# Row maxima and shift of the first causal group inside the project stage, x loaded further ahead, and the local attention's window loop written out

## The chip, the cores and the metric

The kernel runs on one core of one Trainium2 chip. The metric is the device time of one execution in microseconds (us); of several executions the median counts.

## The reference, cut to what matters

The input x has shape (4, 1024, 256). It is normalised, and the normalised rows xn go two ways: through a causal attention of 16 heads of 16 columns, and through two layers of a local attention (window 128, look-back of one window, 8 heads of 64) with a gated feed-forward. The result is x plus the product of the first with silu of the second.

```python
xn = layernorm(x)
s = causal_attention(xn, W_q, W_k, W_v, W_o)
h = xn
for l in range(2):
    h = h + local_attention(shift(h) @ wqkv[l]) @ wo[l]
    a, g = split(norm(shift(h)) @ w1[l] + b1[l])
    h = h + (a * gelu(g)) @ w2[l] + b2[l]
out = x + s * silu(h)
```

Both attentions need, for each row of scores, its maximum before the exponential. What stands below turns on those of the causal attention.

## The kernel before

The program runs stage after stage: `phase_project`, `phase_causal`, then `phase_window` and `phase_feed` for each of two layers. In each stage every engine has its own list of instructions, written out by hand, which it works through strictly in order; semaphores join the lists. A stage is a block: no engine enters the next one before all have left it.

**Project (lines 81 to 360).** The 4096 tokens are cut into 8 supers of 512. For super s, VectorE (DVE) takes moments of the rows of super s + 2 (`moments`, L275, L279) and normalises those of super s + 1 (`normalise`, L285); TensorE (PE) turns the rows (`transposes`, L331), ScalarE (ACT) copies them (L250), and DVE takes the rounding remainder (`lo_of`, L291). Then for each of four groups g of heads PE makes queries and keys with six matmuls into its own bank of `pQ` (L345). These are split into three bf16 parts in a chain: ACT copies the first part (L258), DVE subtracts it (L308, `p_rest`), ACT copies the second (L260), GpSimd (POOL) subtracts the third (L206). After the four groups PE makes the values with 24 matmuls (L356) into `pV`, two banks, which DVE copies out (L317, two copies). The queue of SyncE (SP) stores the parts to `QKP` (L152), the normalised rows to `X` (L146) and the values to `VA` (L157), and loads the rows of super s + 2 (L172). It also fills the operands of the first causal group, `ca_qs`, `ca_ks` and `ca_vin`: 13 transfers (`stack_transfers`), of which four go out after each of supers 2, 3 and 4, and one after super 5 (`first_group`, L167).

**Causal (from line 363).** There are 16 groups, each one batch and four heads. A group needs its 48 row maxima first: a bf16 matmul of up to 512 columns into one of three banks `ca_pR` (`maxima`, L549), then one DVE instruction that keeps the maximum (`take_max`, L691 for a chunk without a mask, L687 with one). `MAXJOBS` lists them: eight query tiles from the last to the first, four heads, one or two chunks of keys. DVE then splits the maxima into two bf16 parts (`split`, L697 to L701), PE turns them (`turn_shift`, L561), DVE copies them out (L706), and two small transfers place them as two extra rows of `ca_qs` (`place_shift`, L508). Only then can PE make scores that already hold the shift (`scores`, L573), of which ACT takes the exponential (L659). For groups 1 to 15 the maxima are spread through the steps of the group before. Those of group 0 stand alone at the head of the stage, in `first`, with the first nine of group 1 (`NEARLY`) behind them. POOL sets `ca_ks`'s two rows of ones and the pad of `ca_va` at the head of the stage (L463 to L467).

**Window (from line 804).** 32 windows per layer. Every engine but DVE runs 24 of them in a loop of three passes over eight windows, and the last eight written out:

```python
    def steps(e, step):
        with e.Fori(0, NW // TPB - 1) as it:
            for j in range(TPB):
                step(it * TPB + j, j, it)
        for j in range(TPB):
            step(NW - TPB + j, j, NW // TPB - 1)
```

DVE has all 32 written out. A pass ends in a branch backwards, so each layer has two. In the windows with j = 0, the first of a batch, the look-back block is left out. PE turns the rows of a later window once in each (`turn_h`, L1230), and opens a window with 18 matmuls (`project`, L1252).

## Time and profile before

| what | us |
|---|---|
| median of 3 executions (1977.71 to 1978.39) | 1978.15 |
| the profiled execution's own time | 1978.07 |
| its span in the trace | 1976.2 |
| project stage and the change of stage, to the first causal matmul | 112.36 |
| from there to the first causal scores | 35.16 |
| causal stage after that, to the first window matmul | 483.6 |
| PE busy | 1839.4 |
| DVE busy | 1502.2 |
| ACT busy | 1208.0 |
| POOL busy | 988.4 |

The own time is what the clock outside measured for the profiled execution; the span reaches from the first to the last instruction in the trace. Busy shares are sums over the whole run. In rows of the trace "L308" is a line of the code, the name left of "<-" is written and those right of it are read, "xN" merges N equal instructions, and what stands in square brackets at the end is the time that the engine sat idle just before and what released it.

### The profile page before, as it was taken

Reading aid. Unit: us, or ns where it says so; the run is one execution under the profiler, and the core shown is the slowest. Engines: PE = TensorE matmul, PEld = TensorE weight load, DVE = VectorE, ACT = ScalarE, POOL = GpSimd, SP = SyncE. Lnnn points to the kernel's source line nnn. Section 1 sums busy time; section 2 is a strip of 40 time slices with the busy share of each in tenths; the row PEclk is TensorE's granted clock in tenths of the full one; section 3 lists DMA queues with packets and bytes.
Section 4 is the critical chain, followed back from the end, with each engine's and each line's share of the span. In section 5 each row is a group of like instructions: output and inputs, shape, how many; then the busy total and the mean of one; then the engine's idle time right before and its main releaser. Section 6 shows DMA issues by size and latency. Waiting matters only on the chain. (4 is left out here: it accounts for less than half of the span.)

```text
span 1976.2 us, 38537 instructions
## 1 busy us (share of the span) xinstructions
PE 1839.4 (93%) x12768; PEld 1314.2 (66%) x12768; DVE 1502.2 (76%) x4131; ACT 1208.0 (61%) x2523; POOL 988.4 (50%) x801
## 2 busy tenths in 40 slices
PE   6879999999998899999997899979999999789999
PEld 5723333333333687878886788868888888668888
DVE  5778888888881998989996555369999999855654
ACT  3516666666666677777775433447777777644553
POOL 3532223222222777767773433357777777443433
PEclk9969999999998899999998999989999999989999
DMA  6993456456430000000022112110000001232222
GB/s 208 308 194 44 66 68 84 60 74 78 59 44 23 14 28 24 25 28 28 28 74 69 61 57 65 44 35 24 26 27 27 27 27 28 63 117 85 71 69 86
DMA packets 142299, 126.87 MB, mean 64 GB/s; under 512 B 31091, under 2 KB 124719, under 8 KB 141999
## 3 DMA queue, kind: packets, MB, share of 16 engines
q1 hardware_dynamic: 140782, 123.36, 27.2%
q8 instruction: 96, 1.57, 0.3%
q10 hardware_dynamic: 1344, 1.31, 0.2%
q14 instruction: 77, 0.62, 0.1%
HBM read 82.41 MB, written 41.96 MB: 63 GB/s over the span
## 5 line engine op out<-in xcount | busy, mean ns | idle before, releaser
L659 ACT ACTIVATE ca_pr<-ca_pS 128x1024 f32<-128x1024 f32 (+3 forms) x384 | 296.6, 811 | 207.2 <-PE ca_pS L573 166.6
L488 POOL TENSOR_SCALAR_AFFINE_SELECT ca_pr<-ca_pr 128x256 f32<-128x256 f32 x256 | 103.7, 409 | 372.9 <-ACT ca_pr L659 368.8
L687 DVE CUSTOM_DVE_ANT_0 ca_masked<-ca_pR,ca_later 128x256 f32<-128x256 f32 (+3 forms) x512 | 235.9, 485 | 43.2 <-PE ca_pR L549 39.4
L549 PE MATMUL ca_pR<-ca_ks,ca_qs 96*128 96x512 bf16 (+3 forms) x768 | 220.6, 345 | 9.1 <-DVEq L743 5.7
L573 PE MATMUL ca_pS<-ca_qs,ca_ks 98*128 98x512 bf16 (+3 forms) x768 | 184.8, 332 | 10.5 <-issue 5.3
L691 DVE TENSOR_REDUCE ca_mx<-ca_pR 128x1 f32<-128x512 f32 x256 | 175.7, 686 | 24.8 <-PE ca_pR L549 23.0
L549 PEld LDWEIGHTS ca_pR<-ca_ks,ca_qs 96*128 96x128 bf16 x768 | 70.7, 98 | 165.0 <-DVE ca_mx L687 90.6
L909 POOL TENSOR_TENSOR wb_tsn<-wb_qk,wb_tab 128x512 f32<-128x512 f32 x62 | 133.4, 2173 | 71.1 <-DVE wb_pn L1127 71.1
L594 PE MATMUL ca_pO<-ca_pr,ca_va 128*32 128x512 f32 (+3 forms) x1536 | 166.0, 504 | 1.2 <-POOL ca_pr L488 0.8
L909 POOL TENSOR_TENSOR w_tsn<-w_qk,w_tab 128x512 f32<-128x512 f32 x62 | 129.0, 2101 | 76.0 <-DVE w_pn L1127 67.3
L985 ACT ACTIVATE w_pe<-w_sm,w_nmax 128x256 f32<-128x256 f32 (+1 forms) x256 | 123.2, 483 | 66.7 <-DVE w_nmax L1117 66.4
L985 ACT ACTIVATE wb_pe<-wb_sm,wb_nmax 128x256 f32<-128x256 f32 (+1 forms) x256 | 123.2, 483 | 63.8 <-DVE wb_nmax L1117 63.8
L573 PEld LDWEIGHTS ca_pS<-ca_qs,ca_ks 98*128 98x128 bf16 x768 | 62.5, 98 | 114.1 <-ACT ca_pr L659 68.2
L1127 DVE TENSOR_SCALAR w_pn<-w_pe,w_rsum 128x256 f32<-128x256 f32 (+1 forms) x256 | 97.2, 442 | 2.3
L1127 DVE TENSOR_SCALAR wb_pn<-wb_pe,wb_rsum 128x256 f32<-128x256 f32 (+1 forms) x256 | 95.9, 437 | 2.3
L917 POOL TENSOR_TENSOR wb_rs<-wb_ssc,mhalf 128x16 f32<-128x16 f32 x32 | 94.0, 2939 | 2.7
L917 POOL TENSOR_TENSOR w_rs<-w_ssc,mhalf 128x16 f32<-128x16 f32 x32 | 93.9, 2936 | 2.7
L1117 DVE CUSTOM_DVE_ANT_0 wb_sm<-wb_pS,masks 128x256 f32<-128x256 f32 (+1 forms) x256 | 88.6, 403 | 8.7 <-PE wb_pS L1348 8.7
L1117 DVE CUSTOM_DVE_ANT_0 w_sm<-w_pS,masks 128x256 f32<-128x256 f32 (+1 forms) x256 | 88.6, 403 | 8.4 <-PE w_pS L1348 8.3
L1252 PE MATMUL w_pX<-big_hi,w_thi 128*128 128x512 f32 x192 | 79.3, 413 | 4.3 <-issue 4.3
L1527 POOL TENSOR_TENSOR f_alo<-f_af,f_ahi 128x512 fp32r<-128x512 f32 x40 | 52.6, 1320 | 61.3 <-ACT f_ahi L1584 61.3
L1527 POOL TENSOR_TENSOR fb_alo<-fb_af,fb_ahi 128x512 fp32r<-128x512 f32 x40 | 52.7, 1323 | 58.1 <-ACT fb_ahi L1584 58.1
(293 smaller groups left out, 5417.7 us busy)
## 6 DMA issues: line engine op xcount, KB each, us to landing
QKP<-p_parts SPq DMA_DIRECT2D x32, 384.0 KB, 5.2
ca_qs<-QKP SPq DMA_DIRECT2D x96, 128.0 KB, 6.5
ca_ks<-QKP SPq DMA_DIRECT2D x96, 128.0 KB, 7.0
w_xt<-X SPq DMA_DIRECT2D x64, 128.0 KB, 2.1
X<-w_x SPq DMA_DIRECT2D x64, 128.0 KB, 1.7
f_hh<-X SPq DMA_DIRECT2D x32, 256.0 KB, 6.2
p_xin<-x SPq DMA_DIRECT2D x8, 512.0 KB, 5.7
X<-p_xn SPq DMA_DIRECT2D x8, 512.0 KB, 4.9
```

The costliest lines, as they stand in the source:

```text
L549: pe.matmul(bank[:, 0:w], qs[0:SHIFT_ROW, u, h, i * P:(i + 1) * P], ks[0:SHIFT_ROW, u, h, k0:k0 + w], start=True, stop=True).then_inc(ring ...
L573: ins = pe.matmul(pS[:, pair, hh, 0:w], ks[:, u, h, j * P:(j + 1) * P], qs[:, u, h, q0:q0 + w], start=True, stop=True)
L594: ins = pe.matmul(pO[h * VW:(h + 1) * VW, o:o + w], va[:, u, j, h * VW:(h + 1) * VW], pr[:, k % 2, h // 2, h % 2, 0:w], start=j == 0, stop ...
L659: act.activation(pr[:, k % 2, pair, :, 0:w], pS[:, pair, :, 0:w], ACT.Exp, scale=CS).then_inc(p_ready, 1)
L687: dve.tensor_tensor_reduce(masked[:, jb % RING, 0:w], pR[jb % RING][:, 0:w], later[:, 512 - w:512], -1.0, BIG, ALU.add, ALU.min, mx[:, i, ...
L691: dve.tensor_reduce(mx[:, i, h, ch:ch + 1], pR[jb % RING][:, 0:w], AX.X, ALU.max, negate=True).then_inc(ring_free, 1)
L909: pool.tensor_tensor(*sines(w, j, z), ALU.mult).then_inc(S["ts_ready"], 1)
L917: pool.tensor_tensor(rs[:, j % 2], ssc[:, :], K.mhalf[:, :], ALU.pow).then_inc(S["rs_ready"], 1)
L985: ins = act.activation(pe_[:, h, 0:keys], sm[:, n, 0:keys], ACT.Exp, bias=nmax[:, n:n + 1], scale=-1.0, accum_out=sums[:, h:h + 1])
L1117: ins = dve.tensor_tensor_reduce(sm[:, n, 0:keys], pS[:, n // 2, n % 2, 0:keys], masks[:, j % 2, 0:keys], -1.0, BIG, ALU.add, ALU.min, nma ...
L1127: ins = dve.tensor_scalar(pn[:, h, 0:keys], pe_[:, h, 0:keys], rsum[:, h:h + 1], None, ALU.mult)
L1527: pool.tensor_tensor(alo[:, j, ch], af[:, ch % 2], ahi[:, j, ch].bitcast(F32), ALU.subtract)\
```

## The change

- In the project stage the 48 maxima of group 0 are made during supers 3 to 7, 10 in each and 8 in the last. They are dealt over the four groups g of a super as 3, 2, 3, 2 (2 each in the last), each lot behind the queries and keys of its g on PE, and behind `p_rest` of its g on DVE. They use the two banks of `pV`. PE waits before the first for all 13 transfers of group 0, before each maximum for the bank to be read by the maximum two before it, and before the value matmuls of a super for all its maxima to be read.
- The two copies of the values out of `pV` move from DVE to ACT, behind the last of the four groups.
- After the last super DVE splits the maxima, PE turns them, DVE copies them, and SP places the two rows.
- SP issues seven of the 13 transfers of group 0 inside super 2 and six behind it, and the same for group 1 at super 4. The causal stage's head then loads group 2 alone.
- x has six blocks for its rows (two of its own, four borrowed from buffers of later stages), and five more supers are loaded at the start.
- POOL sets one slot of the rows of ones after each of supers 0, 1 and 2, and the pad of `ca_va` after super 3.
- `steps` of the window stage has no loop: all 32 windows are written out for every engine, in both layers.

The diff, cut to its core:

```diff
@@ -39,6 +39,8 @@
...
+NJ = len(MAXJOBS)
 LOADS = 2 * len(PAIRS) + 1
 
 LAYERS = 2
@@ -78,9 +80,11 @@
...
-def phase_project(nc, K, W, x, X, QKP, VA, wqk, wv):
-
-    FIRST_AT, FIRST_TURNS = 2, 4
+def phase_project(nc, K, W, F, x, X, QKP, VA, wqk, wv):
+
+    LOAD_AT = {2: 0, 4: 1}
+    MAX_AT = 3
+    PER = {MAX_AT + i: 10 if i < 4 else NJ - 40 for i in range(5)}
@@ -108,7 +112,9 @@
...
-        x_loaded = [sem(f"p1_x_loaded{i}") for i in range(2)]
+        AHEAD = 6
+        x_loaded = [sem(f"p1_x_loaded{i}") for i in range(AHEAD)]
+        blocks = [xin[:, 0], xin[:, 1], F.hh[:, 0], F.hh[:, 1], F.x2[:, 0], F.x2[:, 1]]
...
+
+        def jobs_of(s, g):
+
+            if s not in PER:
+                return []
+            first = sum(PER[i] for i in range(MAX_AT, s))
+            at = [first + -(-PER[s] * i // CG) for i in range(CG + 1)]
+            return range(at[g], at[g + 1])
+
+        def max_bank(idx):
+            return pV[:, idx % 2].rearrange("p n d -> p (n d)")
@@ -133,7 +154,8 @@
...
-            sp.dma_start(xin[:, 1], x_t[1]).then_inc(x_loaded[1], 16)
+            for i in range(1, AHEAD):
+                sp.dma_start(blocks[i], x_t[i]).then_inc(x_loaded[i], 16)
             sp.dma_start(K.base[:, :, :, :], K.tables).then_inc(K.zeroed, 16)
@@ -153,30 +175,34 @@
                                  parts[:, g]).then_inc(part_stored[g], 16)
                     if g == 1 and s + 1 < SUPERS:
                         rows_of(s + 1, 1 - j)
+                    if g == 2 and s in LOAD_AT:
+                        load_group(LOAD_AT[s], 0)
                 sp.wait_ge(v_copied, ONE + 2 + s * 2 + 2)
                 sp.dma_start(va_t[it, j], vst[:, j]).then_inc(v_stored[j], 16)
 
-            def first_group(turn):
+            def load_group(n, turn):
 
...
+                share = -(-LOADS // 2)
+                for transfer in stack_transfers(K, QKP, VA, n, n)[turn * share:(turn + 1) * share]:
+                    sp.dma_start(*transfer).then_inc(K.stacks[4][n], 16)
...
             def rows_of(s, j):
                 store_xn(s, j, s // 2)
-                if s + 2 < SUPERS:
-                    sp.dma_start(xin[:, j], x_t[s + 2]).then_inc(x_loaded[j], 16)
+                if s + AHEAD < SUPERS:
+                    sp.dma_start(blocks[s], x_t[s + AHEAD]).then_inc(x_loaded[s], 16)
 
             def step(s, j, it, final):
                 rest_of(s, j, it)
-                if FIRST_AT <= s < FIRST_AT + FIRST_TURNS:
-                    first_group(s - FIRST_AT)
+                if s in LOAD_AT:
+                    load_group(LOAD_AT[s], 1)
 
             steps(sp, lambda: rows_of(0, 0), step)
+            sp.wait_ge(shift_copied, ONE + 1)
+            place_shift(sp, K, 0)
@@ -207,15 +233,31 @@
...
+                if s < SLOTS:
+                    stack_presets(s)
+                elif s == SLOTS:
+                    value_presets()
+                elif final:
+                    pool.wait_ge(masked, ONE + 8 + SLOTS + 2)
 
...
+            def stack_presets(u):
+                pool.wait_ge(part2, ONE + CG + (u + 1) * CG)
+                pool.memset(ks[SHIFT_ROW:SROWS, u, :, :], 1.0).then_inc(masked, 1)
...
+            def value_presets():
+                heads = K.stacks[3][:, :, :, :].rearrange("p u t (h w) -> p (u t h) w", w=VW)
+                pool.memset(heads[:, :, CD + 1:VW], 0.0).then_inc(masked, 1)
+                pool.memset(heads[:, :, CD:CD + 1], 1.0).then_inc(masked, 1)
@@ -260,19 +302,51 @@
...
+                for v in range(2):
+                    act.wait_ge(v_ready, ONE + s * 2 + v + 1)
+                    if v == 0:
+                        act.wait_ge(v_stored[j], ONE + it * 16)
+                    act.activation(vst[:, j, :, 2 * v:2 * v + 2],
+                                   pV[:, v].rearrange("p n (g c) -> p g n c", g=CG), ACT.Copy).then_inc(v_copied, 1)
...
+            def take_max(idx):
+
+                h, i, ch = MAXJOBS[idx]
+                w = min((i + 1) * P - ch * 512, 512)
+                if idx == 0:
...
+                dve.wait_ge(max_full, ONE + idx + 1)
+                if ch * 512 + w == (i + 1) * P:
+                    dve.sem_inc(K.passed, 1)
+                    dve.tensor_tensor_reduce(masked_to[idx % 2][:, 0:w],
+                                             max_bank(idx)[:, 0:w], K.later[:, 512 - w:512],
+                                             -1.0, BIG, ALU.add, ALU.min, K.mx[:, i, h, ch:ch + 1]).then_inc(max_free, 1)
+                else:
+                    dve.tensor_reduce(K.mx[:, i, h, ch:ch + 1], max_bank(idx)[:, 0:w], AX.X, ALU.max,
+                                      negate=True).then_inc(max_free, 1)
...
+            def split():
+
+                dve.wait_ge(max_free, ONE + 2 + NJ)
@@ -310,12 +384,12 @@
                         moments(s + 2, j, it + 1)
                     if g == CG - 2 and not final:
                         lo_of(s + 1, 1 - j)
-                for v in range(2):
-                    dve.wait_ge(v_ready, ONE + s * 2 + v + 1)
-                    if v == 0:
-                        dve.wait_ge(v_stored[j], ONE + it * 16)
-                    dve.tensor_copy(vst[:, j, :, 2 * v:2 * v + 2],
-                                    pV[:, v].rearrange("p n (g c) -> p g n c", g=CG)).then_inc(v_copied, 1)
+                    for idx in jobs_of(s, g):
+                        take_max(idx)
+                if final:
+                    split()
+                    dve.wait_ge(shift_turned, ONE + 1)
+                    dve.tensor_copy(K.shift[:, :], pT[0:2 * GH, 0].bitcast(BF16)).then_inc(shift_copied, 1)
@@ -331,6 +405,18 @@
...
+            def maxima(s, idx):
+
+                h, i, ch = MAXJOBS[idx]
+                k0 = ch * 512
+                w = min((i + 1) * P - k0, 512)
+                if idx == 0:
+                    pe.wait_ge(K.stacks[4][0], ONE + LOADS * 16)
+                pe.wait_ge(v_copied, ONE + s * 2 + idx % 2 + 1)
+                pe.wait_ge(max_free, ONE + idx + 1)
+                pe.matmul(max_bank(idx)[:, 0:w], qs[0:SHIFT_ROW, 0, h, i * P:(i + 1) * P],
+                          ks[0:SHIFT_ROW, 0, h, k0:k0 + w], start=True, stop=True).then_inc(max_full, 1)
@@ -346,10 +432,14 @@
                     ins.then_inc(q_ready, 1)
                     if g == CG - 2 and not final:
                         transposes(s + 1, 1 - j)
+                    for idx in jobs_of(s, g):
+                        maxima(s, idx)
                 for n in range(SUP):
                     v, o = n // 2, n % 2
                     if o == 0:
                         pe.wait_ge(v_copied, ONE + s * 2 + v + 1)
+                    if n == 0 and s in PER:
+                        pe.wait_ge(max_free, ONE + 2 + jobs_of(s, CG - 1)[-1] + 1)
...
             steps(pe, first, step)
+            pe.wait_ge(split_done, ONE + 3)
+            for i in range(TPB):
+                ins = pe.transpose(pT[0:2 * GH, 0].bitcast(BF16)[:, i * P:(i + 1) * P],
+                                   K.nms[:, i].rearrange("p a h -> p (a h)"), K.identb[:, :])
+            ins.then_inc(shift_turned, 1)
...
+def place_shift(sp, K, u):
+
+    for part in range(2):
+        sp.dma_start(K.stacks[0][SHIFT_ROW + part:SHIFT_ROW + part + 1, u, :, :],
+                     K.shift[part * GH:(part + 1) * GH, :]).then_inc(K.shifted[u], 16)
@@ -459,13 +555,6 @@
...
-            for u in range(SLOTS):
-                pool.memset(ks[SHIFT_ROW:SROWS, u, :, :], 1.0).then_inc(ones, 1)
-                pool.wait_ge(ones, ONE + u + 1)
-            heads = va[:, :, :, :].rearrange("p u t (h w) -> p (u t h) w", w=VW)
-            pool.memset(heads[:, :, CD + 1:VW], 0.0).then_inc(va_preset, 1)
-            pool.memset(heads[:, :, CD:CD + 1], 1.0).then_inc(va_preset, 1)
@@ -514,11 +601,9 @@
...
             def first():
-                for n in range(1, SLOTS):
-                    load(n, n)
+                load(2, 2)
                 load_rows(sp, W, 0, X)
                 load_qkv(sp, W, 0, wqkv)
-                place_shift(0, NJ + NEARLY + 1)
@@ -603,13 +687,9 @@
             def first():
-                pe.wait_ge(loaded[0], ONE + LOADS * 16)
-                for idx in range(NJ):
-                    maxima(idx, 0, 0, (idx, 0))
                 load_wait(1, 0)
                 for idx in range(NEARLY):
-                    maxima(idx, 1, 1, (NJ + idx, 0))
-                turn_shift(0, (NJ + NEARLY, 0))
+                    maxima(idx, 1, 1, (NJ + 1 + idx, 0))
 
             def step(n, u, it, started, more):
@@ -717,12 +795,8 @@
             def first():
-                for idx in range(NJ):
-                    take_max(idx, (idx, 0))
-                split(0, NJ)
                 for idx in range(NEARLY):
-                    take_max(idx, (NJ + idx, 0))
-                take_shift((NJ + NEARLY, 0))
+                    take_max(idx, (NJ + 1 + idx, 0))
@@ -811,16 +888,13 @@
     S = W.sems
     g0 = layer * NW
 
-    def steps(e, step):
-        with e.Fori(0, NW // TPB - 1) as it:
-            for j in range(TPB):
-                step(it * TPB + j, j, it)
-        for j in range(TPB):
-            step(NW - TPB + j, j, NW // TPB - 1)
+    def steps(step):
+        for w in range(NW):
+            step(w, w % TPB, w // TPB)
@@ -1218,8 +1292,7 @@
                 elif late == 1:
                     feed_lo()
 
-            for w in range(NW):
-                step(w, w % TPB, w // TPB)
+            steps(step)
 
         @block.tensor
         def _(pe):
...
```

The rest of the diff passes the moved tiles and semaphores along and drops the tests that told a loop's window from a written one.

**DVE, project stage, around the third and fourth group of super 4** (`p_rest` is the split's subtraction, `p_xn` the normalised rows, `p_tlo` the remainder of the turned rows, `p_vst` the values' copy; "ISA" that writes `ca_mx` is the masked maximum, with a short read-out behind it). Before, from the first group of that super:

```order
L308 TENSOR_TENSOR p_rest<-p_pQ,p_parts 128x512
L285 TENSOR_SCALAR p_xn<-p_xin,p_mv,p_rstd 128x256 x4
L308 TENSOR_TENSOR p_rest<-p_pQ,p_parts 128x512 x2
L275 BN_STATS p_stt<-p_xin 128x6 x4
L279 BN_AGGR p_mv<-p_stt 128x2 x4
L291 TENSOR_TENSOR p_tlo<-p_pT,p_thi 128x1024
L308 TENSOR_TENSOR p_rest<-p_pQ,p_parts 128x512
L317 COPY p_vst<-p_pV 128x4x128 x2
L308 TENSOR_TENSOR p_rest<-p_pQ,p_parts 128x512
```

Now, from the third group's `p_rest` on:

```order
L382 TENSOR_TENSOR p_rest<-p_pQ,p_parts 128x512
L349 BN_STATS p_stt<-p_xin 128x6 x4
L353 BN_AGGR p_mv<-p_stt 128x2 x4
L365 TENSOR_TENSOR p_tlo<-p_pT,p_thi 128x1024
L330 ISA w_x,ca_mx<-p_pV,ca_later 128x384
L330 ISA ca_mx 128x1
L334 TENSOR_REDUCE ca_mx<-p_pV 128x1
L330 ISA w_x,ca_mx<-p_pV,ca_later 128x256
L330 ISA ca_mx 128x1
L382 TENSOR_TENSOR p_rest<-p_pQ,p_parts 128x512
L334 TENSOR_REDUCE ca_mx<-p_pV 128x1
L330 ISA w_x,ca_mx<-p_pV,ca_later 128x256
```

The value copies are gone from DVE, and three maxima stand between `p_tlo` and the last `p_rest`.

**PE, project stage, the last group of a super** (`p_pT` takes the turned rows, `p_pQ` queries and keys, `p_pV` the values and now also the scores of which the maxima are taken). Before:

```order
L331 MATMUL p_pT<-ident,p_xn 128x128 x8
L345 MATMUL p_pQ<-p_thi,big_hi 128x512
L345 MATMUL p_pQ<-p_tlo,big_hi 128x512
L345 MATMUL p_pQ<-p_thi,big_lo 128x512
L345 MATMUL p_pQ<-p_thi,big_hi 128x512
L345 MATMUL p_pQ<-p_tlo,big_hi 128x512
L345 MATMUL p_pQ<-p_thi,big_lo 128x512
L356 MATMUL p_pV<-big_hi,p_thi 128x256
L356 MATMUL p_pV<-big_lo,p_thi 128x256
```

Now, in super 3:

```order
L405 MATMUL p_pT<-ident,p_xn 128x128 x8
L417 MATMUL p_pV<-ca_ks,ca_qs 128x512 x3
L431 MATMUL p_pQ<-p_thi,big_hi 128x512
L431 MATMUL p_pQ<-p_tlo,big_hi 128x512
L431 MATMUL p_pQ<-p_thi,big_lo 128x512
L431 MATMUL p_pQ<-p_thi,big_hi 128x512
L431 MATMUL p_pQ<-p_tlo,big_hi 128x512
L431 MATMUL p_pQ<-p_thi,big_lo 128x512
L417 MATMUL p_pV<-ca_ks,ca_qs 128x512
L417 MATMUL p_pV<-ca_ks,ca_qs 128x384
L446 MATMUL p_pV<-big_hi,p_thi 128x256
```

Three maxima stand ahead of the last group's queries and keys, and two between them and the values.

**SP, project stage, super 2** (`QKP`, `X` and `VA` are the stores, `ca_qs` and `ca_ks` the operands of the causal group). Before, from the super's first stores:

```order
L152 DMA QKP<-p_parts 384x1x512 x2
L146 DMA X<-p_xn 128x4x256
L172 DMA p_xin<-x 128x4x256
L152 DMA QKP<-p_parts 384x1x512 x2
L157 DMA VA<-p_vst 128x4x256
L167 DMA ca_qs<-QKP 16x4x1024
L167 DMA ca_ks<-QKP 16x4x1024
L167 DMA ca_qs<-QKP 16x4x1024
L167 DMA ca_ks<-QKP 16x4x1024
L152 DMA QKP<-p_parts 384x1x512 x2
```

Now:

```order
L174 DMA QKP<-p_parts 384x1x512 x2
L168 DMA X<-p_xn 128x4x256
L174 DMA QKP<-p_parts 384x1x512
L191 DMA ca_qs<-QKP 16x4x1024
L191 DMA ca_ks<-QKP 16x4x1024
L191 DMA ca_qs<-QKP 16x4x1024
L191 DMA ca_ks<-QKP 16x4x1024
L191 DMA ca_qs<-QKP 16x4x1024
L191 DMA ca_ks<-QKP 16x4x1024
L191 DMA ca_qs<-QKP 16x4x1024
L174 DMA QKP<-p_parts 384x1x512
L181 DMA VA<-p_vst 128x4x256
```

Seven loads stand ahead of the super's last store of parts and of its values' store; six more follow behind these.

## Rows read from the trace of the kernel before

**Rows 1.** The page's 40 slices of the span: TensorE's granted clock in tenths

```profile
PEclk9969999999998899999998999989999999989999
```

**Rows 2.** Stretches: us; busy PE, PEld, DVE, ACT, POOL; clock; DMA share; GB/s

```profile
56.30:100.50 44.20, 38.50 (x226) 32.30 (x225) 33.24 (x69) 22.13 (x36) 22.82 (x23) 1.00 1.03 319
100.50:112.36 11.86, 6.20 (x40) 5.41 (x39) 3.96 (x6) 3.98 (x7) 6.56 (x6) 0.85 0.72 251
112.36:147.52 35.16, 28.62 (x66) 6.67 (x67) 29.77 (x97) 0.00 (x0) 10.74 (x6) 0.50 1.05 174
...
760.50:764.40 3.90, 3.88 (x10) 3.12 (x11) 3.75 (x10) 0.79 (x3) 0.99 (x1) 0.56 0.20 59
```

**Rows 3.** Timeline of DVE, super 5: start us, us, engine, line, operation, [idle before]

```profile
79.10 0.69 DVE L308 TENSOR_TENSOR p_rest<-p_pQ,p_parts 128x512 f32<-128x512 f32 x1 [1.18 <-ACT p_parts L258]
79.71 2.21 DVE L285 TENSOR_SCALAR p_xn<-p_xin,p_mv,p_rstd 128x256 f32<-128x256 f32 x4
81.84 0.68 DVE L308 TENSOR_TENSOR p_rest<-p_pQ,p_parts 128x512 f32<-128x512 f32 x1
83.77 0.69 DVE L308 TENSOR_TENSOR p_rest<-p_pQ,p_parts 128x512 f32<-128x512 f32 x1 [1.26 <-ACT p_parts L258]
...
87.33 0.68 DVE L308 TENSOR_TENSOR p_rest<-p_pQ,p_parts 128x512 f32<-128x512 f32 x1
87.92 1.28 DVE L317 COPY p_vst<-p_pV 128x512 f32<-128x512 f32 x2
89.99 0.69 DVE L308 TENSOR_TENSOR p_rest<-p_pQ,p_parts 128x512 f32<-128x512 f32 x1 [0.79 <-ACT p_parts L258]
```

**Rows 4.** PE, super 5: a group's first of six matmuls; values' first, last

```profile
82.82 0.47 PE L345 MATMUL p_pQ<-p_thi,big_hi 128*128 128x512 f32 x1
...
84.28 0.28 PE L356 MATMUL p_pV<-big_hi,p_thi 128*128 128x256 f32 x1
...
86.91 0.28 PE L356 MATMUL p_pV<-big_hi,p_tlo 128*128 128x256 f32 x1
```

**Rows 5.** Timeline of DVE, head of the causal stage

```profile
112.98 0.69 DVE L691 TENSOR_REDUCE ca_mx<-ca_pR 128x1 f32<-128x512 f32 x1 [4.97 <-PE ca_pR L549]
...
136.22 0.19 DVE L697 TENSOR_TENSOR ca_nm<-ca_mx 128x32 f32<-128x32 f32 x1
...
142.28 0.68 DVE L706 COPY ca_shift<-ca_pR 8x1024 bf16<-8x1024 bf16 x1
```

**Rows 6.** PE, head of the causal stage: turned shift, first scores

```profile
141.23 1.01 PE L561 MATMUL ca_pR<-identb,ca_nms 128*8 128x128 bf16 x8
147.52 1.01 PE L573 MATMUL ca_pS<-ca_qs,ca_ks 98*128 98x512 bf16 x2 [5.28 <-issue]
```

**Rows 7.** Timeline of SP's queue, super 2: issues

```profile
52.93 4.06 SPq L152 DMA_DIRECT2D QKP<-p_parts  x2
...
57.77 0.50 SPq L167 DMA_DIRECT2D ca_qs<-QKP  x1
```

**Rows 8.** DMA issues, 50 to 80: KB each, median us from issue to landing

```profile
ca_qs<-QKP SPq DMA_DIRECT2D x5, 128.0 KB, 6.0
```

**Rows 9.** Timeline of ACT, super 3: a first part and its wait

```profile
67.18 0.60 ACT L258 ACTIVATE p_parts<-p_pQ 128x512 bf16<-128x512 f32 x1 [1.37 <-DMA QKP<-p_parts]
```

**Rows 10.** Timeline of POOL at the head of the causal stage

```profile
110.60 10.64 POOL L463 MEMSET ca_ks<- 2x4096 bf16 x3 [1.89 <-POOLq L85]
```

**Rows 11.** PE around the first branch of each layer; L1230 once a window

```profile
755.19 0.33 PE L1230 MATMUL w_pX<-ident,w_xt 128*128 128x128 f32 x1
...
760.52 0.56 PE L1252 MATMUL w_pX<-big_hi,w_thi 128*128 128x512 f32 x1 [2.17 <-issue]
...
770.54 0.30 PE L1230 MATMUL w_pX<-ident,w_xt 128*128 128x128 f32 x1 [0.71 <-issue]
...
1415.22 0.33 PE L1230 MATMUL wb_pX<-ident,w_xt 128*128 128x128 f32 x1
...
1427.28 0.30 PE L1230 MATMUL wb_pX<-ident,w_xt 128*128 128x128 f32 x1 [0.71 <-issue]
```

More of the change, by code:

```diff
@@ L41 @@
 SLOTS = 3
+MAXJOBS = [(h, i, ch) for i in range(TPB - 1, -1, -1) for h in range(GH) for ch in range(1 + i // 4)]
+NJ = len(MAXJOBS)
 LOADS = 2 * len(PAIRS) + 1
@@ L366, in phase_causal @@
     RING = 3
-    MAXJOBS = [(h, i, ch) for i in range(TPB - 1, -1, -1) for h in range(GH) for ch in range(1 + i // 4)]
-    NJ = len(MAXJOBS)
     PER = [6, 3, 6, 3, 6, 4, 5, 3, 3, 0, 0, 0]
@@ L440, in phase_causal @@
         pO = ps("ca_pO", [P, 512], F32)
-        ones = sem("ca_ones")
-        shifted = [sem(f"ca_shifted{i}") for i in range(SLOTS)]
         ring_full, ring_free = sem("ca_ring_full"), sem("ca_ring_free")
@@ L502, in load, with put_shift @@
                     sp.dma_start(*transfer).then_inc(loaded[u], 16)
-            def place_shift(u, jobs):
+            def put_shift(u, jobs):
                 sp.wait_ge(ring_free, ONE + RING + jobs)
-                for part in range(2):
-                    sp.dma_start(qs[SHIFT_ROW + part:SHIFT_ROW + part + 1, u, :, :],
-                                 shift[part * GH:(part + 1) * GH, :]).then_inc(shifted[u], 16)
+                place_shift(sp, K, u)
             def store(n, half, jobs):
@@ L628, in do @@
                             turn_out(n - which, which, (job, n))
-                if not started:
-                    pe.wait_ge(ones, ONE + SLOTS)
                 pe.wait_ge(shifted[u], ONE + (it + 1) * 2 * 16)
@@ L890, in step @@
             def step(w, j, it):
[L891 removed]
+                if w == NW - 4:
                     start_feed()
@@ L1279, in attend @@
             def attend(w, j, it):
-                last = min(w + 3, NW) if isinstance(w, int) else w + 3
+                last = min(w + 3, NW)
                 nxt = ahead(w, j, it, 1)
@@ L1310, in turn_k @@
             def turn_k(w, j, it):
-                last = min(w + 2, NW) if isinstance(w, int) else w + 2
+                last = min(w + 2, NW)
                 pe.wait_ge(S["qkn_ready"], ONE + g0 + w + 1)
@@ L1319, in turn_q @@
             def turn_q(w, j, it):
-                last = min(w + 2, NW) if isinstance(w, int) else w + 2
+                last = min(w + 2, NW)
                 pe.wait_ge(S["v_copied"], ONE + g0 + last)
```

72 lines of the change are left out of this document (42 added, 30 removed).

## The prediction

> **What bounds the kernel now.** I read the strip of TensorE's clock first, then the stretches of the stages that change, then the timelines of the engines there, and last the DMA issues.
>
> The strip [rows 1] shows TensorE at 0.8 to 1.0 of full speed everywhere but in the fourth slice, which reads 0.6. The stretches [rows 2] place that dip in the head of the causal stage: 35.16 us at a granted clock of 0.50, with PE counted busy for 28.62 and DVE for 29.77. There one DVE instruction after another makes the maxima. The timeline of DVE [rows 5] shows the first at 112.98 and the split at 136.22: 48 maxima in 23.24 us, 0.484 each. Behind the split nine early maxima of group 1 and the turn come, the shift is copied at 142.28, and the first scores follow at 147.52 behind an idle PE [rows 6].
>
> The project stage is of another kind. Supers 3 to 6 [rows 2] last 44.20 us, 11.05 each. In that time PE is busy for 38.50, DVE for 33.24, and the DMA share is 1.03. DVE's timeline of one super [rows 3] shows a chain between engines in each group of heads: `p_rest` frees ACT, ACT's next first part frees the next `p_rest`, one every 1.9 us. From 79.10 to 89.99 DVE waits 1.18 and 1.26 us for ACT. PE fits its value matmuls (24 of them from 84.28 to 86.91 and the length of one, 2.75 us) into time in which DVE makes moments and remainder [rows 4]. So the slack that the new maxima would use is there by its sum, 2.7 us of DVE in a super; the question is whether the order of the lists can reach it.
>
> **The change, term by term.** The sum is made against the profiled execution's own 1978.07 us, 0.08 below the median of the three runs. A measurement of this kernel can tell some 0.2%, 4 us, from no change.
>
> *Head of the causal stage.* The 48 maxima, the split and the wait for the placed shift leave. Nine early maxima stay: 9 x 0.484 = 4.4, and 0.3 to the first scores. From 35.16 [rows 2] to 4.7: **-30.5**. The placing of the shift is hidden by these nine (142.28 to 147.52 was 5.2, of which the stage change takes part).
>
> *Values' copies on ACT.* They took DVE 1.28 [rows 3]. On ACT they stand ahead of the next super's first part, which waits for that engine 0.4 us per super in supers 1 to 3, where nothing else is longer: **+1.3**. From super 4 on it is inside the turn below. DVE gains 1.28 a super, already counted there.
>
> *The wait for the 13 transfers.* PE waits for all of group 0 before the first maximum, which stands in super 3 right behind the queries and keys of its first group. These end about 1.2 us after the `p_rest` at 56.30, so PE is there at 57.5. SP issues the seven loads inside super 2 between the two stores of parts that now span 52.93 to 57.0 [rows 7]. At 0.50 us an issue the seven are out at about 58, then the store of parts and the values' store take 2.4, then six more: about 64. A load of 128 KB lands 6.0 us after its issue [rows 8], which makes 70. Below that only if these loads did not queue; above it, since the DMA share is 1.03 already and nine more loads than now fall into this place. Bounds 68 and 73; I take 70.5, nearest to the row's 6.0. Everything else on PE is queued behind that wait: the next groups' queries and keys, and with them ACT, DVE and the stores. **+13** (10.5 to 15.5). In the trace of before ACT waits for stores already, 1.37 at 67.18 [rows 9]; that wait disappears under the new one.
>
> *The turn of a super.* This is the largest term. Two banks hold three maxima in a lot, so PE's third waits until DVE has read the first, and what is behind it on PE waits too; and the values wait until DVE has read the super's last maximum, in the same two banks. Per super, from one `p_rest` to the next:
> - first group: `p_rest` 0.6, three maxima 1.5, `p_xn` 2.1 [rows 3]: 4.2;
> - second: two maxima fit beside the chain: 1.9;
> - third: `p_rest` 0.6, moments and remainder 2.95 (84.38 to 87.33), first maximum 0.5, PE's third 0.24, six matmuls 1.37 (1.46 with the first's start [rows 4]) and 0.16 to their end, ACT's first part 0.6 [rows 9]: 6.45;
> - fourth: `p_rest` 0.6, two maxima 1.05, then on PE values 2.75, and the next super's queries and keys 1.53, ACT 0.6: 6.5.
>
> That is 19.1, and with the hand-overs 19.2, for 11.05: 8.15 more, four times: **+32.6**. What lay side by side on PE and DVE is one behind the other: values and queries of the fourth group (4.1 us) can't start before the maxima are read, the maxima can't before `p_rest`.
>
> *Last super.* It has no `p_xn`, moments or remainder, and its two maxima a group fit the chain. But values start when its last maximum is read, then PE turns the shift (1.01 [rows 6]), DVE copies it (0.68 [rows 5]), and SP issues two placings, 0.6 each: **+3** (2 to 5).
>
> *The clock.* The dip at 0.50 leaves with the maxima's head. But the new turn has PE idle for some 3.8 us in front of the third group's third maximum. In the window stage PE sat idle for 2.17 before 760.52 [rows 11], and the 3.90 us from there ran at 0.56 [rows 2], between the levels of 1.2 and 2.4 GHz: 3.90 x 0.44 = 1.7 us lost per drop. The 5.7 us that PE is idle in supers 3 to 6 now, in many short pieces, left the clock at 1.00 [rows 2]. One drop a super: **+6.7** (0; or, if PE stays at the lower level, twice 1.37 and 2.75 on the path doubled in each of four turns, +22).
>
> *The window loop.* PE turns its rows once a window [rows 11]. Around the first branch of layer 0 the two stand 15.35 us apart (755.19 to 770.54), around that of layer 1 only 12.06 (1415.22 to 1427.28). A pass has the same work, so a branch cost 3.3 in layer 0 and nothing in layer 1; the second of each layer is like its first. Twice 3.3: **-6.5**. Here a rule of the Trainium skill speaks otherwise: "Runtime: NRT & Kernel Launch", section "Instruction fetch mechanics", says that a taken branch to code outside the two pages held forces a fetch before execution goes on. By that rule all four branches would pay, and the sum would be 6.6 lower. The row of layer 1 shows no such stall, so I go by the rows; the rule stays as a rival.
>
> *Priced at nothing.* POOL's three fills of ones, 3.5 each [rows 10], stand behind supers 0 to 2. POOL is busy for 22.82 of 44.20 [rows 2], idle for 5.3 a super in four pieces, the longest about one link of the chain, 1.9. The other 1.6 makes a store of parts later, which ACT would feel only if that store had no slack, once per fill (0 to 4.8). x further ahead: no `moments` waited for x beyond the start, so nothing is gained; five loads at the start share the DMAs with the weights (0 to 2).
>
> Sum: -30.5 + 1.3 + 13 + 32.6 + 3 + 6.7 - 6.5 = +19.6, and 1978.07 + 19.6 = **1997.7 us**.
>
> **Rivals.**
> - *The clock holds.* PE waits in pieces and none lets it fall: the sum without 6.7, **1991**. For it: the idle pieces of the project stage drop nothing now. Against: 2.17 in one piece did.
> - *The clock stays low* over supers 3 to 6: +22 for +6.7, **2013**. For it: at 0.50 the head of the causal stage ran with PE busy in 81% of the time, and the new turn has it busy for about 60%.
> - *Every branch pays* as in layer 0, so that writing out saves 13.2: **1991**.
> - *Writing out saves nothing*, since the stall was that of code arriving and comes back at the same place: **2004.2**. For it: only the layer with code not run lately paid.
> - *The maxima find DVE's slack*: faster. The place is the pair of banks. If values and the next queries could run beside DVE's maxima, a turn would be DVE's own work: 8.3 in place (33.24 / 4), less 1.3 of copies, and ten maxima of 0.5 with hand-overs, 13.0 in all. If moreover the 13 loads had landed by 57.5, the wait would be nothing. Then 1.3 + 4 x 1.95 + 3 - 30.5 - 6.5 = -25: **1953**. It decides whether a turn is below about 17 us with the loads' wait below 3: there the sum crosses zero. For it: DVE has 2.7 us of idle time a super. Against: the written order puts PE's waits ahead of that work.
> - *Half of each*: turn 16 us and a wait of 8, no clock loss: 1.3 + 8 + 19.8 + 3 - 30.5 - 6.5 = -4.9, near **no change**.
>
> **How the numbers follow.** The forecast as summed has 0.55. The clock that holds 0.13, the clock that stays low 0.07, every branch 0.05, no saving from the unrolling 0.05, the packed maxima 0.11, half of each 0.04. Faster by over 0.2% is the packed case, 0.11; within 0.2% is the half case, 0.04; slower is the rest, 0.85. The range takes in the wait's bounds (2.5 each way), the case of 1991 less these and the smaller terms' slack (1984), and that of 2013. It leaves out the packed case, the half case and the upper tail of the low clock: under 0.2.
>
> **What would show it.** Right: PE in super 3 idle for about 13 us with the loads of group 0 as releaser, ending near 70; `p_rest` to `p_rest` of supers 3 to 6 at about 19 us; DVE's `p_tlo` followed by a maximum with PE's third maximum behind it, then the matmuls; the first causal matmul near 112.36 + 56.6 = 169; the first scores 5 us after the first maximum of the causal stage; in layer 0 12.06 at each turn of the window stage. Wrong: a turn of 13 to 15 us, or loads that land before PE arrives, would make the kernel faster than I say; a clock row of 0.5 over the whole of supers 3 to 6 slower.

## The result

| | changed | before, beside it |
|---|---|---|
| median, us | 2008.49 (2006.71 to 2009.46, 4 runs) | 1977.93 (1971.93 to 1978.39, 4 runs) |
| ratio | 1.016 (95% interval 1.0146 to 1.0175) | |
| profiled execution, us | 2009.46, span 2007.7 | 1978.07, span 1976.2 |

The change costs 1.6%, some 31 us. One execution of the last experiment below took 2257.97 us at a mean granted clock of 0.741, and its ratio leaves it out. The strip of the clock and five stretches of the changed kernel, with the columns of [rows 2]:

```profile
PEclk8778999999999899999999999989999999899999
```

```profile
60.50:76.46 15.96, 0.57 (x3) 0.14 (x2) 0.69 (x1) 2.20 (x5) 5.82 (x3) 0.59 1.07 206
77.18:100.61 23.43, 17.09 (x67) 12.08 (x66) 12.34 (x32) 6.39 (x10) 6.19 (x7) 0.71 0.23 81
100.61:165.11 64.50, 43.03 (x201) 32.65 (x202) 33.95 (x92) 20.71 (x33) 16.42 (x16) 0.81 0.57 151
165.11:181.39 16.28, 10.04 (x56) 7.88 (x55) 7.08 (x24) 5.27 (x9) 5.26 (x5) 0.83 0.44 156
181.39:186.18 4.79, 4.79 (x9) 0.94 (x10) 4.17 (x10) 0.00 (x0) 0.00 (x0) 0.50 1.07 142
```

The single dip to 0.6 (it is the third slice in [rows 1]; the prediction miscounts it as the fourth, and its place in time, 112 to 147, stands) has become 0.7 in the second and third. The first causal matmul comes at 181.39, not 112.36: the project stage is 69.0 us longer. The head of the causal stage, from there to the first scores, is 4.79 for 35.16. Supers 3 to 6 (62.10 to 165.11) take 103.0 for 44.2, at a DMA share of 0.23 and 0.57, for 1.03 before, once the loads are done. The first stretch is a wait, seen on PE, whose timeline goes on with super 3:

```profile
76.46 1.03 PE L417 MATMUL p_pV<-ca_ks,ca_qs 96*128 96x512 bf16 x2 [15.39 <-DMA ca_vin<-VA]
...
89.33 0.38 PE L417 MATMUL p_pV<-ca_ks,ca_qs 96*128 96x512 bf16 x1 [3.75 <-DVE ca_mx L330]
...
93.97 0.55 PE L446 MATMUL p_pV<-big_hi,p_thi 128*128 128x256 f32 x1 [1.80 <-DVE ca_mx L330]
...
98.29 0.28 PE L446 MATMUL p_pV<-big_hi,p_tlo 128*128 128x256 f32 x1
98.40 0.39 PE L431 MATMUL p_pQ<-p_thi,big_hi 128*128 128x512 f32 x1
```

PE idles 15.39 us for the 13th transfer, 3.75 in front of the third group's third maximum, and 1.80 in front of the values, which then take 4.43 (93.97 to 98.40) for 2.75 with the rows of [rows 4]. The first `p_rest` of supers 4 to 7 on DVE:

```profile
100.61 0.69 DVE L382 TENSOR_TENSOR p_rest<-p_pQ,p_parts 128x512 f32<-128x512 f32 x1 [6.79 <-ACT p_parts L300]
...
123.29 0.69 DVE L382 TENSOR_TENSOR p_rest<-p_pQ,p_parts 128x512 f32<-128x512 f32 x1 [7.83 <-ACT p_parts L300]
...
144.93 0.69 DVE L382 TENSOR_TENSOR p_rest<-p_pQ,p_parts 128x512 f32<-128x512 f32 x1 [6.82 <-ACT p_parts L300]
...
165.11 0.69 DVE L382 TENSOR_TENSOR p_rest<-p_pQ,p_parts 128x512 f32<-128x512 f32 x1 [5.16 <-ACT p_parts L300]
```

Turns of 22.7, 21.6 and 20.2 us stand for 11.05 before. DVE's idle time grew from 1.2 in front of that row [rows 3] to 5 to 8.

The window loop shows what was forecast. The rows turned at the first place of the branch in layer 0, 12.05 apart where [rows 11] have 15.35:

```profile
791.94 0.33 PE L1303 MATMUL w_pX<-ident,w_xt 128*128 128x128 f32 x1
803.99 0.30 PE L1303 MATMUL w_pX<-ident,w_xt 128*128 128x128 f32 x1 [0.71 <-issue]
```

One thing stands in no term of the forecast's sum. The timelines of DVE and POOL in super 1:

```profile
34.59 5.82 DVE L359 TENSOR_SCALAR p_xn<-f_hh,p_mv,p_rstd 128x256 f32<-128x256 f32 x4
```

```profile
35.17 3.54 POOL L254 MEMSET ca_ks<- 2x4096 bf16 x1
```

The four instructions of `p_xn` took 5.82 us; one of them alone 3.68, as long as the fill of ones beside it. In the kernel before the same four took 2.45. Super 3 begins at 62.10 instead of 56.30, 5.8 later, where I had 1.3.

### The profile page after: what moved, and what is told of

Same layout as the page of the kernel before. It is cut to its first block and busy times, and to the rows that moved or that the text cites. A ratio compares the mean times of both kernels' runs of the same rounds, so it can differ in the third digit from the quotient of the medians.

```text
span 2007.7 us, 37379 instructions
## 1 busy us (share of the span) xinstructions
PE 1836.5 (91%) x12768; PEld 1319.7 (66%) x12768; DVE 1498.0 (75%) x4115; ACT 1214.9 (61%) x2537; POOL 995.8 (50%) x801
## 3 DMA queue, kind: packets, MB, share of 16 engines
q1 hardware_dynamic: 140782, 123.36, 26.9%
## 5 line engine op out<-in xcount | busy, mean ns | idle before, releaser
L765 DVE CUSTOM_DVE_ANT_0 ca_masked<-ca_pR,ca_later 128x512 f32<-128x512 f32 (+1 forms) x480 | 221.1, 485 | 36.8 <-PE ca_pR L634 34.3
L634 PE MATMUL ca_pR<-ca_ks,ca_qs 96*128 96x512 bf16 (+1 forms) x720 | 197.1, 334 | 6.5 <-DVEq L817 4.2
L769 DVE TENSOR_REDUCE ca_mx<-ca_pR 128x1 f32<-128x512 f32 x240 | 164.8, 687 | 22.6 <-PE ca_pR L634 20.8
L983 POOL TENSOR_TENSOR w_tsn<-w_qk,w_tab 128x512 f32<-128x512 f32 x62 | 135.9, 2212 | 67.7 <-DVE w_pn L1201 67.7
L634 PEld LDWEIGHTS ca_pR<-ca_ks,ca_qs 96*128 96x128 bf16 x720 | 65.5, 97 | 144.5 <-DVE ca_mx L765 81.3
L232 POOL TENSOR_TENSOR p_parts<-p_rest,p_parts 128x512 bf16<-128x512 f32 x32 | 37.0, 1159 | 94.5 <-ACT p_parts L302 86.0
```

What stands on the lines that cost most here:

```text
L634: pe.matmul(bank[:, 0:w], qs[0:SHIFT_ROW, u, h, i * P:(i + 1) * P], ks[0:SHIFT_ROW, u, h, k0:k0 + w], start=True, stop=True).then_inc(ring ...
L765: dve.tensor_tensor_reduce(masked[:, jb % RING, 0:w], pR[jb % RING][:, 0:w], later[:, 512 - w:512], -1.0, BIG, ALU.add, ALU.min, mx[:, i, ...
L769: dve.tensor_reduce(mx[:, i, h, ch:ch + 1], pR[jb % RING][:, 0:w], AX.X, ALU.max, negate=True).then_inc(ring_free, 1)
L983: pool.tensor_tensor(*sines(w, j, z), ALU.mult).then_inc(S["ts_ready"], 1)
```

## The experiments

Times of the edited kernels are medians; where I compare two of them, I go by the ratios to the kernel before, measured beside each. The intervals of these ratios reach 2.2 to 2.9 us to each side for the loop alone and the last two kernels, and 3.4 to 5 us for the others, so a difference of two of them is known to some 5 us. A time of "first scores" is read from each profile, 186.18 in the changed kernel and 147.52 before.

**The loop alone** (kernel before with the window loop written out):

```diff
-        with e.Fori(0, NW // TPB - 1) as it:
-            for j in range(TPB):
-                step(it * TPB + j, j, it)
-        for j in range(TPB):
-            step(NW - TPB + j, j, NW // TPB - 1)
+        for w in range(NW):
+            step(w, w % TPB, w // TPB)
```

> The kernel before with only the window loop written out. Theory (a branch costs 3.3 us in layer 0 and nothing in layer 1): 6.5 us less than before, about 1971.5; the rows of the turned h stand 12.06 apart at both places of layer 0. Rival (code fetch comes back at another place, or every branch pays): 0, or 13 less.

Measured: 1973.24, ratio 0.9977 (0.9966 to 0.9988), so 4.5 us less (2.4 to 6.7). Its rows:

```profile
754.47 0.33 PE L1227 MATMUL w_pX<-ident,w_xt 128*128 128x128 f32 x1
766.51 0.30 PE L1227 MATMUL w_pX<-ident,w_xt 128*128 128x128 f32 x1 [0.71 <-issue]
```

12.04 for 15.35. The rows give 6.5, the runs hold it in their interval, and both rivals lie outside it, nothing saved and all four branches paid (13.2).

**The fills behind supers 4 to 6:**

```diff
-                if s < SLOTS:
-                    stack_presets(s)
+                if SLOTS < s <= 2 * SLOTS:
+                    stack_presets(s - SLOTS - 1)
...
```

> The changed kernel, with POOL's three fills of ones moved from behind supers 0, 1, 2 to behind supers 4, 5, 6, where DVE is idle. Theory: the fill at 35.17 holds DVE's normalise (one of its four instructions took 3.68 us instead of about 0.5) and POOL's next third part, and through them the store, ACT and super 2: super 3 starts near 58 instead of 62.10 and the kernel takes 4 us less, about 2004.5. Rival (late only by the new x loads and copies of the values on ACT): 0 to 1 less, super 3 still at 61 to 62.

Measured: 1999.94, ratio 1.0113 (1.0096 to 1.013), 9 us less than the change. In super 1 `p_xn` takes 2.48 again. Super 3 starts at 58.21, 3.9 earlier, as expected; first scores at 178.51, 7.7 earlier. The other half comes from the turns (super 4's is 21.2 for 22.7, the last super 14.7 for 16.3), which I had not expected and did not take apart.

**Ten maxima dealt 5, 5, 0, 0:**

```diff
+            deal = (1, 1, 0, 0)
-            at = [first + -(-PER[s] * i // CG) for i in range(CG + 1)]
+            at = [first + -(-PER[s] * sum(deal[:i]) // sum(deal)) for i in range(CG + 1)]
...
```

> The changed kernel, with the ten maxima of a super dealt 5, 5, 0, 0 over the groups instead of 3, 2, 3, 2. Theory (the turn is long since values wait for the last group's maxima and the last group's queries for the third group's first maximum): the turn from the first p_rest to the next falls from 21.5 to about 16 to 17, 18 us less in all, about 1990. Rival (the turn is the sum of DVE's work, or the DMAs): turns stay at 20 or more, less than 4 us gained.

Measured: 1999.47, ratio 1.0116 (1.0099 to 1.0134). In its profile (an execution of 1991.75, where the other three took 1998.18 to 2001.06) the turns of supers 4, 5 and 6 are 17.2, 16.9 and 19.5, and first scores come at 172.15, 14 earlier. So the same ten maxima cost 5.5, 4.7 and 0.7 us less a turn where they don't stand ahead of the values and of the last queries. By the runs 9 of the forecast 18 arrived, by the profile 14: the direction is shown, the size only to some 5 us. PE's waits in these turns are at most 1.8 us after the first, and the clock from 77 to 150.6 is 0.84, so part of the gain is the clock's, which this run doesn't separate.

**PE kept busy in its waits:**

```diff
...
+                        if i == 2 and g == CG - 2:
+                            idle_matmuls(s, CG - 1, j, 14)
                         maxima(s, idx)
+                if s in PER and not final:
+                    idle_matmuls(s + 1, 0, j, 7)
```

> The changed kernel, with PE given 14 matmuls into the bank of the next queries and keys ahead of the third group's third maximum, and 7 ahead of the values, in supers 3 to 6, where it only waits; their results are overwritten. Theory (half speed behind these waits costs 2 to 3 us a turn): the values are made in 2.75 us instead of 4.4 to 5.3, turns fall by 2.5 each, 10 us less, about 1998.5. Rival (the clock is not on the path, or the extra matmuls outlast the wait): 0, or up to 4 us more.

Measured: 1997.77, ratio 1.0106 (1.0086 to 1.0127), 11 us less than the change (some 5 to each side), though PE does more. The values of super 3 and the stretch of 77 to super 7:

```profile
92.15:95.06 2.91, 2.91 (x25) 2.91 (x26) 0.00 (x0) 0.60 (x1) 2.17 (x3) 1.00 0.36 129
77.00:157.44 80.44, 71.21 (x351) 53.92 (x352) 45.81 (x124) 27.35 (x43) 22.75 (x23) 0.93 0.51 145
```

The values take 2.91 at a clock of 1.00, where they took 4.43 at 0.61, and the whole runs at 0.93. In the profiles the turn of super 3 is 2.6 shorter, counted from the end of PE's wait, those of supers 4 and 5 are 3.6 and 1.4 shorter, that of super 6 is 0.6 longer, and the first scores come at 176.89, 9.3 earlier. The gain isn't even since the loss wasn't: in the changed kernel the values ran at half speed throughout in super 4 (0.50), in part in supers 3 and 5, and in super 6 not at all (1.00). Super 4 now turns in 19.1:

```profile
97.28 0.69 DVE L382 TENSOR_TENSOR p_rest<-p_pQ,p_parts 128x512 f32<-128x512 f32 x1 [5.28 <-ACT p_parts L300]
...
116.41 0.69 DVE L382 TENSOR_TENSOR p_rest<-p_pQ,p_parts 128x512 f32<-128x512 f32 x1 [5.16 <-ACT p_parts L300]
```

So the half speed behind the waits cost some 10 us.

**One super later** (`MAX_AT = 4`, 10, 10, 10 and 18 maxima):

> The changed kernel, with the maxima in supers 4 to 7 (10, 10, 10, 18) instead of 3 to 7. Theory (PE's wait for the 13 transfers is 15 us of nothing, since they land at 76.4 whoever waits): super 3 runs as before the change, PE waits at most 2 us at super 4, the last super is some 4 longer; 20 us less in all, about 1988. Rival (the transfers are slow since the DMAs are full, and land only later when stores run beside them): they land past 80, PE waits over 6 us, 10 less at most.

Measured: 2000.25, ratio 1.0108 (1.0091 to 1.0125), 10 us less, half of what I expected. PE's row at super 4, and the stretch of super 3:

```profile
76.08 0.60 PE L417 MATMUL p_pV<-ca_ks,ca_qs 96*128 96x512 bf16 x2 [0.51 <-DMA ca_vin<-VA]
```

```profile
62.66:77.75 15.09, 10.79 (x56) 8.61 (x54) 9.45 (x18) 6.58 (x11) 10.08 (x9) 0.89 1.08 234
```

The wait is gone and the transfers land when they did. But super 3 takes 15.1, not 11.05, for two reasons. The third fill now stands beside its `p_xn`, which takes 4.15 for 2.2. And thirteen loads in one place hold up the stores of parts, with the DMAs full: ACT waits 2.05 for one at 77.12. And the last super, with 18 maxima, takes 27.1 (141.98 to 169.03), 10.8 more than with 8, where I had put 4. PE's next queries stand behind four or five maxima in two banks; that this is the whole of it wasn't tested.

**All 48 in super 7** (`MAX_AT = 7`, `PER = {7: NJ}`, `LOAD_AT = {2: 0, 7: 1}`, the fills behind supers 4 to 6):

> The changed kernel, with all 48 maxima in super 7 (12 behind each group), group 1 loaded in super 7 instead of 4, and the fills behind supers 4 to 6. Theory (wait and turns are gone, and the maxima cost their own 0.5 to 0.55 each, as at the head of the causal stage before): super 7 starts at 102 to 104, first scores near 147 to 150, so 1972 to 1976. Rival (two banks pace the maxima at 0.7 and more, with PE at half speed): 8 us later, 1981 to 1985.

Measured: 1996.36, ratio 1.0092 (1.0075 to 1.0109), 20 us above the theory's 1976 and 11 above the rival's 1985. Super 7 starts at 112.17, not 102 to 104. Part of that is again the burst of loads: super 3 takes 15.9 with no fill beside it, 11.5 before, and ACT waits 0.77 and 4.64 in it for stores of parts. Part is the fills, which here no long turn covers. DVE and POOL in supers 5 and 6:

```profile
85.60 4.22 DVE L359 TENSOR_SCALAR p_xn<-p_xin,p_mv,p_rstd 128x256 f32<-128x256 f32 x4
...
99.21 4.13 DVE L359 TENSOR_SCALAR p_xn<-p_xin,p_mv,p_rstd 128x256 f32<-128x256 f32 x4
```

```profile
84.29 3.51 POOL L254 MEMSET ca_ks<- 2x4096 bf16 x1
...
97.81 3.51 POOL L254 MEMSET ca_ks<- 2x4096 bf16 x1
```

The slow `p_xn` has moved with the fills. The 48 maxima with four hand-overs take 40.6 (112.78 to 153.4), and PE then waits for group 1, which left late since it stands behind the stores:

```profile
168.81 5.02 PE L634 MATMUL ca_pR<-ca_ks,ca_qs 96*128 96x512 bf16 x9 [9.77 <-DMA ca_vin<-VA]
```

**The fills beside the maxima** (that kernel with all three fills behind super 6):

> The kernel with all 48 maxima in super 7, with the three fills together behind super 6, beside the maxima, instead of behind supers 4, 5 and 6. Theory (a fill stops only DVE instructions from SBUF to SBUF, as the normalise; a maximum read from PSUM is not stopped): normalise in supers 5 and 6 takes 2.2 us again instead of 4.2, turns 11.1 instead of 13.6, maxima as fast as before, 5 us less, about 1991. Rival (a fill stops any DVE instruction): up to 10 us more in super 7, so 5 more.

Measured: 1991.13, ratio 1.0084 (1.0065 to 1.0102). The medians are 5.2 apart, as expected, but the ratios only 1.6, so the times show no gain. The profiles do:

```profile
86.87 2.22 DVE L360 TENSOR_SCALAR p_xn<-p_xin,p_mv,p_rstd 128x256 f32<-128x256 f32 x4
...
97.87 2.21 DVE L360 TENSOR_SCALAR p_xn<-p_xin,p_mv,p_rstd 128x256 f32<-128x256 f32 x4
```

```profile
107.95 10.63 POOL L255 MEMSET ca_ks<- 2x4096 bf16 x3
```

`p_xn` takes 2.2 again, and super 7 starts at 108.15, 4.0 earlier. The fills stand beside the 12 maxima of the first group. An unmasked one takes 0.69 there as elsewhere, and the 48 take as long as in the kernel above, where a fill stood only beside the first few: from the first unmasked one to the last 26.9 us, and 26.6 there. A fill stops the normalise, and not a maximum that is read from PSUM.

**Both: fills behind supers 4 to 6, and 5, 5, 0, 0:**

> The changed kernel with two edits together: the fills behind supers 4 to 6, and the ten maxima of a super dealt 5, 5, 0, 0. Theory (the two costs are separate): by the first scores, which came 7.7 us earlier with the one and 14.0 with the other, the sum of 21.7, so first scores at about 165 and about 1987 in all. Rival (they share a cost, the half-speed values): 15 at most, 1993.

Measured: 1993.58, ratio 1.0085 (1.0065 to 1.0105), first scores at 170.15, 16.0 earlier for the sum of 21.7. That speaks for the rival, that the two gains overlap, but doesn't show it: 14.0 of the 21.7 come from a profile 8 us below the median of its kernel, and by the ratios the two save 9.3 and 8.7, together 18.0, and both at once 14.8, a difference within the noise.

**Values' copies back on DVE:**

> The changed kernel, with the copies of the values back on DVE. Theory (on ACT they stand ahead of the next first part in supers 1 to 3, and in the long turns they are hidden behind PE's queries): 1 us less, about 2007.5; super 2 and 3 start 0.4 earlier each. Rival (DVE's 1.3 a super is on the path of the turn): 5 more.

Measured: 2010.07, ratio 1.0152 (1.0131 to 1.0174): no difference that these runs can tell. Super 3 starts at 62.69 and the first scores come at 186.95. But super 2 starts at 49.13 instead of 50.40, so on ACT the copies did cost 1.3 there. Starting earlier, its `p_xn` then met more of the second fill:

```profile
49.73 4.18 DVE L353 TENSOR_SCALAR p_xn<-f_hh,p_mv,p_rstd 128x256 f32<-128x256 f32 x4
```

In the changed kernel the same four took 2.92. The fill hid what the copies cost.

**x in two blocks:**

> The changed kernel, with x in two blocks again, super s + 2 loaded after super s. Theory (nothing waited for x): only the start moves, first moments at 4.83 instead of 5.37, 0.5 us less, about 2008. Rival (x taken out of the crowded supers 2 to 4 let the 13 transfers land earlier): they land 1.5 to 3 later, 2 us more.

Measured: 2009.51, ratio 1.0161 (1.0136 to 1.0187): the same. `p_xn` of super 1 takes 5.82 here too, from the block of before, so it isn't x's new place that slows it. PE's wait is 17.23 instead of 15.39, which is the rival's sign, but the first scores come at 182.41, 3.8 earlier, which speaks against it. No effect can be told.

**Eight early maxima, the rest where they were** (on the loop alone; 2 behind group 1 of super 6, 2 behind each of groups 0 to 2 of super 7):

```diff
+    JOBS = {(6, 1): (0, 1), (7, 0): (2, 3), (7, 1): (4, 5), (7, 2): (6, 7)}
...
-                for idx in range(NJ):
+                for idx in range(8, NJ):
```

> The kernel before with the window loop written out, and 8 of the 48 maxima made in the project stage where DVE only waits: 2 behind group 1 of super 6, 2 behind each of groups 0, 1, 2 of super 7; 40 stay at the head of the causal stage. Values' copies stay on DVE, the 13 transfers as before the change. Theory (a maximum costs nothing where no list behind it is late): 8 x 0.484 less than with the loop alone, 3.5 to 3.9 us, about 1969.5; first scores near 144. Rival (values and their store wait for the maxima even so): 0 less, the causal stage begins 2 to 4 later.

Measured: 1979.47, ratio 1.0015 (1.0003 to 1.0027): 7.5 us worse than the loop alone. PE's timeline names two causes:

```profile
97.63 1.03 PE L364 MATMUL p_pV<-ca_ks,ca_qs 96*128 96x512 bf16 x2 [5.77 <-DMA ca_vin<-VA]
...
153.75 0.59 PE L610 MATMUL ca_pS<-ca_qs,ca_ks 98*128 98x512 bf16 x1 [7.79 <-issue]
```

PE waited 5.77 us for the one transfer, of values, that no maximum reads. And where the head is shorter, the two placings (issued at 146.71) come right behind the three loads of window weights (139.65 to 145.5); the first scores follow 7.0 us after, where it was 4.5 before (142.98 to 147.52).

**Six early maxima, weights behind the placings:**

```diff
+    JOBS = {(7, 0): (0, 1), (7, 1): (2, 3), (7, 2): (4, 5)}
...
+                place_shift(0, NJ + NEARLY + 1)
                 load_qkv(sp, W, 0, wqkv)
-                place_shift(0, NJ + NEARLY + 1)
...
```

> The kernel before with the window loop written out, 6 of the 48 maxima made in super 7 (2 behind each of groups 0, 1, 2, none in super 6, so that no wait for the 13 transfers stops PE), and at the head of the causal stage the two placings of the shift issued ahead of the three loads of window weights. Theory (in the kernel with 8 early maxima PE lost 5.77 us to the last of the 13 transfers, ca_vin, which no maximum reads, and the placings 7.8 us behind the weights' loads): both waits leave, super 7 starts at 100 to 102, first scores 2 us behind the turned shift's placing, near 142 to 143 instead of 146.5; 3 to 4 us less than with the loop alone, about 1969.5. Rival (the DMAs are full with loads of groups 1 and 2 and rows, the placings land late all the same): first scores at 146, nothing gained on the loop alone.

Measured: **1969.42, ratio 0.9958 (0.9944 to 0.9973)**, faster than both kernels.

```profile
143.27 1.01 PE L610 MATMUL ca_pS<-ca_qs,ca_ks 98*128 98x512 bf16 x2 [3.50 <-issue]
```

Super 7 starts at 100.86, the placings are issued at 140.52, and the first scores follow 2.75 us behind, 4.25 earlier than before. Of this result the loop is the larger part. Against the loop alone the ratios give 3.8 us (3.6 to each side), barely clear of noise. The profile of the loop alone has its placings at 141.87 and its first scores at 146.53, 4.66 behind them. So of 3.3 us to the first scores 1.9 come from the order of placings and weights, and 1.35 from what lies before the placings, the six maxima among it. No run has either edit by itself.

## Why the prediction was right, and where its terms were off

Forecast 1997.7 (1984 to 2013), slower with 0.85; measured 2008.49. The mechanism held and the sum was 11 short: 31 us slower where 19.6 was forecast. The measured time lies in the range by its upper part, which was there for the rival with a low clock, and it is nearer to that rival's 2013 than to the sum. By terms, all from the profile of the changed kernel, unless said otherwise:

- *Head of the causal stage*: -30.4 for -30.5. *Unrolling*: -6.5 for -6.5, and only in layer 0. Here the page "Runtime: NRT & Kernel Launch", section "Instruction fetch mechanics", of the Trainium skill speaks of branches to code outside the pages held; whether the start of this loop lay outside them no trace shows. Read as I read it, all four branches would pay 13.2; the runs of the loop alone exclude that.
- *The wait for the 13 transfers*: from the end of `p_rest` to the first maximum 14.4 for 13; PE itself idle 15.39. The last landed at 76.4 for 70.5: its issue was at 66.7 for 64, since super 2 was late, and it took 9.8 from issue to landing, where I had taken 6.0 from the smaller loads [rows 8]. One super later confirms that it is a wait for them, and with all 48 in super 7 the burst costs some 4 us even where nobody waits for it.
- *The turn and the clock* together: 103.0 less 44.2 and less 14.4 is 44.4, for 32.6 + 6.7 = 39.3. The structure is the one worked out: 3.75 idle in front of the third maximum (3.8 in the text), the values behind the last maximum. The term that was short is the clock's, "one drop a super". Above the forecast turn of 19.2 the four took 4.9, 3.5, 2.4 and 1.0 more (super 3 without its 14.4), 11.8 for the 6.7 priced. I priced a drop at 1.7. In super 3 the values alone lost 1.7, in super 4 they took 5.26 for 2.75, and the queries ahead of them lost too: from the third `p_rest` to the fourth 7.5 us passed for 6.45. With PE kept busy super 4 turned in 19.1, as the structure says, and the runs gave back 11 us. Supers 5 and 6 turned in 20.3 and 20.8 there; what they lost stays open. One small term went the other way: `p_xn` took 1.37 for 2.1.
- *Last super*: 4.4 for 3.
- *Before super 3*: 5.8 for 1.3. Here a step failed: "POOL's three fills ... stand behind supers 0 to 2", priced at nothing, with POOL's own lateness as the only way it could cost. The fills cost 3.9 up to super 3, since they stop DVE's normalise: in super 1 the next `p_rest` follows `p_xn` without a pause, and ACT waits 5.22 for it. By the first scores their place cost 7.7; how the other half arises wasn't taken apart. What is left before super 3 without them, 1.9, is near the 1.3 that I had charged to the copies on ACT.

The rivals: the packed maxima (0.11) are excluded, the turns being 20 to 24 us. The clock low all the time (0.07) came nearer than I gave it: 0.71 and 0.81 in supers 3 to 6, where the forecast had one short drop a super and that case half speed throughout.

## What to carry to other kernels

Idle time of an engine can be filled only where no in-order list behind it gets a new wait. Ten maxima a super came close to DVE's idle time by their sum (my estimate was a turn of 13.0 for 11.05) and doubled the turn by their place, with what the clock lost behind the new waits. Six, in the one super that had room, cost nothing that shows, and saved about 1 us, which these runs can't tell from nothing. Ask of a wait for a count of transfers which of them the work reads, and of a shortened stage which queue it now ends behind.
